# An AdaLN block and a quantised two-layer network on one core: b1 loaded as two rows, filling products in the prologue, and new orders on every engine

## The reference

```python
# conditional part, x: (2, 1024, 256), cond: (2, 128)
w_down = down_project * (cond @ down_gamma)[:, None, :] + (cond @ down_beta)[:, None, :]
w_up   = up_project   * (cond @ up_gamma)[:, None, :]   + (cond @ up_beta)[:, None, :]
y = relu(x @ w_down) @ w_up + x

# quantised network, F = 1024
def bitlinear(x, w, b):
    xq = act_quant(rmsnorm(x))     # 8 bits, one scale a token
    wq = weight_quant(w)           # -1, 0, 1 times mean(abs(w))
    return xq @ wq.T + b
h = gelu(bitlinear(y, w1, b1))
out = x + bitlinear(h, w2, b2)
```

## Time and profile before

| | us |
|---|---|
| median of 3 runs | 77.22 |
| lowest and highest run | 75.25, 78.56 |
| the profiled execution | 75.27 |
| its span (first to last instruction) | 73.5 |
| TensorE, VectorE, ScalarE, POOL busy | 63.8, 58.1, 55.1, 56.5 |

### The profile page before, as it was taken

The page is one execution under the profiler, slowest core; times in us unless marked ns, Lnnn a source line. Parts: engine busy times, 40 slices in busy tenths (PEclk is TensorE's granted clock), DMA queues, the critical chain, the costliest instruction groups (busy, mean ns, idle before and its releaser), DMA issues.

```text
span 73.5 us, 1375 instructions
## 1 busy us (share of the span) xinstructions
PE 63.8 (87%) x412; PEld 34.9 (47%) x412; DVE 58.1 (79%) x126; ACT 55.1 (75%) x113; POOL 56.5 (77%) x134
## 2 busy tenths in 40 slices
PE   3449995798999999999999999998969998699950
PEld 1042534442733422554355574834416757598830
DVE  4104357998199999799999999999999699999550
ACT  0060157994499949889999999999999999995300
POOL 6700098998889896888879899888899999899700
PEclk9999999955999999999999999999999999999998
DMA  0899999999904004436737709797997996530352
GB/s 6 263 351 288 379 406 430 419 406 428 406 40 92 16 0 89 90 58 123 133 65 143 143 15 270 147 89 167 222 198 145 181 271 118 167 143 16 144 205 73
DMA packets 20478, 13.49 MB, mean 184 GB/s; under 512 B 17748, under 2 KB 18260, under 8 KB 20088
## 3 DMA queue, kind: packets, MB, share of 16 engines
q1 hardware_dynamic: 20256, 12.69, 64.2%
q10 hardware_dynamic: 216, 0.73, 2.9%
HBM read 7.02 MB, written 2.10 MB: 124 GB/s over the span
## 4 chain that ended last, share of the span: by engine, by line
PE 51%; POOL 12%; ACT 11%; DMA 8%; DVE 7%; issue 5%; ACTq 2%; DVEq 0%; POOLq 0%
PE h L325 14%; PE ob L360 12%; DMA b1f<-b_rows 8%; ACT junk_g L481 6%; PE up_ps L302 5%; PE h L333 5%; PE up_ps L293 5%; ACT g L476 5%; POOL b1f L864 3%; DVE q L654 3%; PE ob L252 3%; PE ob L358 2%; POOL b_high L861 2%; PE up_ps L344 2%; ACTq L493 2%
## 5 line engine op out<-in xcount | busy, mean ns | idle before, releaser
L633 DVE TENSOR_REDUCE gtop<-g 128x1 f32<-128x1024 f32 x16 | 19.2, 1207 | 0.7 <-ACT g L476 0.7
L476 ACT ACTIVATE g<-h,ydeq 128x1024 f32<-128x1024 f32 x16 | 17.8, 1127 | 0.2
L481 ACT ACTIVATE junk_g<-g 128x1024 bf16<-128x1024 f32 x16 | 17.1, 1081 | 0.0
L325 PE MATMUL h<-w1q,q1t 128*128 128x512 f16 x64 | 16.5, 380 | 0.0
L360 PE MATMUL ob<-w2q,q2t 128*128 128x256 f16 x128 | 16.3, 272 | 0.0
L360 PEld LDWEIGHTS ob<-w2q,q2t 128*128 128x128 f16 x128 | 12.5, 98 | 1.4
L654 DVE TENSOR_SCALAR q<-g,gm 128x1024 f16<-128x1024 f32 x16 | 11.8, 750 | 0.1
L852 POOL TENSOR_TENSOR x<-x,b 128x512 f32<-128x512 f32 x8 | 10.1, 1271 | 0.0
L325 PEld LDWEIGHTS h<-w1q,q1t 128*128 128x128 f16 x64 | 5.6, 97 | 7.0 <-issue 2.8
L661 DVE SCALAR_TENSOR_TENSOR x<-ob,gdeq,x 128x256 f32<-128x256 f32 x16 | 7.5, 478 | 1.4 <-PE ob L360 1.4
L462 ACT ACTIVATE q<-up_ps,ym 128x256 f16<-128x256 f32 x16 | 6.8, 481 | 0.4 <-DVE ym L629 0.4
(11 more groups left out here) (104 smaller groups left out, 102.6 us busy)
## 6 DMA issues: line engine op xcount, KB each, us to landing
w<-w_t SPq DMA_DIRECT2D x4, 512.0 KB, 7.7
x<-x_tok SPq DMA_DIRECT2D x2, 1024.0 KB, 13.1
out<-x SPq DMA_DIRECT2D x7, 256.0 KB, 2.3
xd<-x_dim SPq DMA_DIRECT2D x1, 1024.0 KB, 13.0
pk<-first_pack ACTq DMA_DIRECT2D x1, 640.0 KB, 4.2
xd<-x_dim SPq DMA_DIRECT2D x1, 512.0 KB, 9.5
xd<-x_dim SPq DMA_DIRECT2D x1, 256.0 KB, 7.6
out<-x SPq DMA_DIRECT2D x2, 128.0 KB, 1.7
```

What stands on the lines that cost most here:

```text
L325: pe.matmul(h_ps[s][:, cols], q1t[:, j, s * DK + c, :], w1q[:, c, cols], start=(i == 0), stop=False)
L476: a.activation(g[:, j % RING, s, :], h_ps[s][:, :], ACT.Gelu, scale=ydeq[:, j, s:s + 1])\
L481: a.activation(junk_g[:, j % 3, s, :], g[:, j % RING, s, :], ACT.Square, scale=F ** -0.5, accum_out=gmean[:, j, s:s + 1]).then_inc(gsq_don ...
L633: v.tensor_reduce(gtop[:, j, s:s + 1], g[:, j % RING, s, :], AX.X, ALU.max, apply_absolute_value=True)\
```

## The change

Four things.

1. **b1.** The host gives b1 as two rows of 512. One load (ACT's queue, first in it) brings them to `b1`, 2 x 512. `spread_b1`, a 2 x 128 pattern of ones that POOL makes early (one memset, one copy), is the stationary operand of a 32-bit product `spread_rows`, which puts the rows on their partitions in `ob[:, 0]`. `split_b1` is now VectorE's and reads that PSUM tile; it stands between VectorE's `down_weights` and `up_weights`. The memset of `b1f` and POOL's `split_b1` are gone.
2. **Loads.** `first_pack` is issued by SP right behind `down_pack`, no longer by ACT.
3. **Filling products.** `keep_warm` calls in the prologue go from 11 products to 18.
4. **Orders.** The lists of all five engines are changed. `gelu(j, s)` for j of 4 and more now also waits for `square_g` and `quantise_g` of the pair that used its place in the ring. POOL's functions can work on several pairs at once (`CHAINS`), but every chain holds one pair; `BY_POOL` is empty, so every `quantise_g` stays on VectorE.

```diff
 LAST = PAIRS - 1
+CHAINS = [(0, 1), (1, 2), (2, 3), (3, 4), (4, 5), (5, 6), (6, 7), (7, 8)]
+CHAIN_OF = [n for n, (a, b) in enumerate(CHAINS) for k in range(a, b)]
+BY_POOL = []
...
         w2s = sb("w2s", [P, D], F16)
+        b1 = sb("b1", [2, HALF])
...
 
             sp.dma_start(dpk[:], down_pack).then_inc(dpk_in, 16)
...
+            sp.dma_start(pk[:], first_pack).then_inc(pk_in, 16)
             for k in range(DK):
                 sp.dma_start(w1[:, k], w1_t[:, k]).then_inc(w1_in[k], 16)
...
+            turn_q2(0, 1)
             turn_q1(3)
-            turn_q2(0, 1)
             turn_q1(4)
             turn_q2(1, 0)
+            store(0)
+            turn_q1(5)
             turn_q2(1, 1)
             turn_q2(2, 0)
-            store(0)
-            turn_q1(5)
             turn_q2(2, 1)
-            turn_q1(6)
             store(1)
             turn_q2(3, 0)
+            turn_q1(6)
             turn_q2(3, 1)
+            store(2)
+            turn_q2(4, 0)
             turn_q1(7)
-            turn_q2(4, 0)
             turn_q2(4, 1)
             turn_q2(5, 0)
-            store(2)
+            store(3)
             turn_q2(5, 1)
-            store(3)
...
+                pe.wait_ge(spread_set, 2)
+                pe.wait_ge(b1_in, 16)
+                pe.matmul(ob[:, 0, :], spread_b1[:, :], b1[:, :], start=True, stop=True).then_inc(b1_spread, 1)
 
             def up_weights():
...
             down_weights()
-            keep_warm(2)
+            spread_rows()
+            keep_warm(1)
             up_weights()
             down(0)
             x_tokens(0)
+            keep_warm(1)
             up(0)
             keep_warm(3)
             down(1)
+            keep_warm(2)
             weight_sum(0)
+            keep_warm(3)
             x_tokens(1)
             up(1)
             keep_warm(3)
             down(2)
             transpose_q1()
+            keep_warm(2)
             x_tokens(2)
+            up(2)
             weight_sum(1)
-            up(2)
             first_layer(0, 0)
+            first_layer(0, 1)
             column_sums()
-            first_layer(0, 1)
             x_tokens(3)
...
+            sum_w2()
             first_layer(2, 0)
-            sum_w2()
             first_layer(2, 1)
             x_tokens(5)
             up(5)
+            second_layer(0, 0)
+            second_layer(0, 1)
             first_layer(3, 0)
-            second_layer(0, 0)
             first_layer(3, 1)
             x_tokens(6)
             up(6)
             first_layer(4, 0)
-            second_layer(0, 1)
+            first_layer(4, 1)
             second_layer(1, 0)
-            first_layer(4, 1)
             x_tokens(7)
             up(7)
             second_layer(1, 1)
-            second_layer(2, 0)
             first_layer(5, 0)
             first_layer(5, 1)
+            second_layer(2, 0)
             second_layer(2, 1)
+            second_layer(3, 0)
             first_layer(6, 0)
             first_layer(6, 1)
-            second_layer(3, 0)
-            first_layer(7, 0)
             second_layer(3, 1)
             second_layer(4, 0)
+            first_layer(7, 0)
+            second_layer(4, 1)
             first_layer(7, 1)
-            second_layer(4, 1)
             second_layer(5, 0)
             transpose_q2(6, 0)
+            transpose_q2(6, 1)
             second_layer(5, 1)
-            transpose_q2(6, 1)
             transpose_q2(7, 0)
...
                 a.wait_ge(ffn1_done, SLOTS * j + s + 1)
                 if s == 0:
-                    a.wait_ge(ydeq_done, j + 1)
+                    a.wait_ge(ydeq_done, CHAIN_OF[j] + 1)
+                if j >= RING:
+                    a.wait_ge(gsq_done, SLOTS * (j - RING) + s + 1)
+                    g_quantised(a, j - RING, s)
                 a.activation(g[:, j % RING, s, :], h_ps[s][:, :], ACT.Gelu, scale=ydeq[:, j, s:s + 1])\
                     .then_inc(gelu_done, 1)
...
-            a.dma_start(pk[:], first_pack).then_inc(pk_in, 16)
-            a.wait_ge(b1_zero, 1)
-            for r in range(4):
-                a.dma_start(b1f[32 * r + 1:32 * r + 10, :], b1_rows[r % 2]).then_inc(b1_in, 16)
+            a.dma_start(b1[:], b1_rows).then_inc(b1_in, 16)
             a.preload_act_table(ACT.Gelu)
             relu(0)
             absolute_sum(0)
             square_y(0)
             relu(1)
             quantise_y(0)
+            round_weights(0)
             absolute_sum(1)
-            round_weights(0)
             square_y(1)
             quantise_y(1)
...
             square_y(2)
             gelu(0, 0)
             quantise_y(2)
             gelu(0, 1)
             square_g(0, 0)
-            relu(3)
+            round_weights(1)
             square_y(3)
             quantise_y(3)
+            relu(3)
             gelu(1, 0)
             gelu(1, 1)
             square_y(4)
+            quantise_y(4)
             gelu(2, 0)
-            quantise_y(4)
             square_g(0, 1)
             gelu(2, 1)
+            square_g(1, 0)
...
             quantise_y(5)
             gelu(3, 0)
-            square_g(1, 0)
+            square_g(1, 1)
             gelu(3, 1)
-            square_g(1, 1)
             square_y(6)
...
+            square_g(3, 1)
+            gelu(5, 1)
+            square_g(4, 0)
             quantise_y(7)
-            gelu(5, 1)
-            square_g(3, 1)
-            square_g(4, 0)
+            square_g(4, 1)
             gelu(6, 0)
-            square_g(4, 1)
+            gelu(6, 1)
             square_g(5, 0)
-            gelu(6, 1)
-            gelu(7, 0)
             square_g(5, 1)
             square_g(6, 0)
+            gelu(7, 0)
             square_g(6, 1)
             square_g(7, 0)
...
+            def split_b1():
+                v.wait_ge(b1_spread, 1)
+                v.wait_ge(part_set, 5)
+                for n, rows in enumerate((ob[:, 0, :], b1f[:, :])):
+                    if n:
+                        v.wait_ge(b1_rest, n)
+                    v.tensor_scalar(b1_high[:, :], upper_half(rows), part[:, n:n + 1], 0.0, ALU.mult, ALU.add)\
+                        .then_inc(b1_upper, 1)
+                    v.wait_ge(b1_upper, n + 1)
+                    v.tensor_tensor(b1f[:, :], rows, b1_high[:, :], ALU.add).then_inc(b1_rest, 1)
...
             v.memset(warm[:], 0.0).then_inc(warm_set, 1)
-            v.memset(b1f[:], 0.0).then_inc(b1_zero, 1)
             v.memset(part[:], 0.0).then_inc(part_set, 1)
...
             down_weights()
+            split_b1()
             up_weights()
```

190 lines of the change are left out of this document (102 added, 88 removed).

## The result

The changed kernel took 79.44 us (median of 4 executions, 78.44 to 106.13) against 77.38 for the kernel before, executed beside it. The ratio is 1.043, with a 95% interval of 1.029 to 1.058: slower. The profiled execution of the changed kernel took 78.81 (span 77.0), that of the kernel before 75.27 (span 73.5).

The account below looks back on a forecast made before the run. Bound: a prologue of waits to 20 us (b1f's load, POOL's split), then full engines. Gains of 1.7 at 20 us, 1.4 at the last gelu, about 1.5 at the end: 75.7 on the median's footing, forecast 75.3, range 73.1 to 77.5.

Parts of the forecast that it names:

- The loads: Start of the prologue: down_pack lands at 3.0 instead of 4.62, and b1 at 3.
- spread_rows: TensorE's prologue: the added 32-bit product of 512 columns takes 0.9 us and is done at 4.9.
- TensorE's own queue ahead of up(0): Prologue: wu ready at 8.4 to 8.6, gain 0.8 us, with the seven more filling products lying in TensorE's waits.
- The gain at 20 us: End of the prologue: first_layer(0, 0) starts at 18.5 against 20.2, a gain of 1.7 us.
- The clock: TensorE from 14.9 to 18.3: fillers hold the clock at 1.00 instead of 0.50, saving 1.0 us on down(2), just hidden.
- rival 2: Whole kernel: the clock spreads the runs, and slower ones vanish with TensorE busy from 3 us; 73 to 74.8, chance 0.22.
- Passes through full engines undiminished: Main part: what is won ahead of 20 us reaches the end through the full engines without loss.
- SP's order: Main part, SP's queue: stores hold back transposes behind them, but turn_q1(7) comes about 52, no later than quantise_y(7) allows.
- POOL's order: Main part, POOL's queue: with b2's additions and chain_g(3) ahead, inverse_y(7) ends near 53, when turn_q1(7) is due.
- ScalarE between 20 and 40: Sign of being right: ScalarE's idle time there stays about as now, 1.6 us.
- signs named as wrong the last: Main part: last gelu under 0.7 us earlier though first_layer(0, 0) is 1.7 us earlier, so new orders lose the prologue's gain.
- The slower rival: Prologue: b1 lands late and delays up_weights and down(0); landing at 6.7 gives 78.3, 1.1 us slower; chance 0.10.
- rival 3: Half the gain is lost to a fixed down_pack time, a falling clock or new waits; 76.4 to 77.3, chance 0.23.

Follow-up runs that it names:

- g11: The kernel before with first_pack issued by SP behind down_pack and seven more filling products, nothing else; 77.12 us in one execution.
- h17: The same kernel as e4, measured again in five rounds; 74.73 us, ratio 0.993 to the kernel before.
- e4: The kernel before, all five lists as they were, with the new b1 path, first_pack on SP and the 18 filling products; 75.96 us.
- f7: The changed kernel with turn_q2(1, 1) ahead of store(0) and turn_q1(5), and add_b2(5), add_b2(6) and chain_g(3) behind inverse_y(7); 76.33 us.
- h15: f7 measured again in five rounds; 76.10 us, ratio 1.014 to the kernel before.
- h13: f7 with the prologue's order swaps on TensorE, ScalarE, VectorE and POOL undone too; 75.55 us, ratio 1.002 to the kernel before.
- g10: f7 with the old path of b1, four loads on ScalarE's queue and the split on POOL; 76.90 us.
- h18: h13 with add_b2(4) moved behind chain_g(3) and add_b2(7) moved behind chain_g(4); 75.89 us.
- e1: The changed kernel with POOL's whole list as in the kernel before; 80.04 us.
- e3: The changed kernel with both POOL's and SP's whole lists as in the kernel before; 80.97 us.
- f6: The changed kernel with only add_b2(5), add_b2(6) and chain_g(3) moved behind inverse_y(7) on POOL; 78.24 us in one execution.
- h14: h13 with sum_w2 back behind first_layer(2, 0) and quantise_y(4) back behind gelu(2, 0); 78.67 us, ratio 1.048.

## Why the prediction was wrong

It said 75.3, with 0.07 for slower by over 2%. Step by step:

- **The loads: right.** down_weights start at 2.84 (3.0 predicted), b1 is no wait.
- **spread_rows: mis-sized.** The term was 0.9 us, half of L235's 1.79 for "four instructions (two products)"; it took 2.07. The misreading is of the overlap. The views by line give the duration of each instruction, spread_rows and then up_weights of the changed kernel, then up_weights of the kernel before:

```profile
L251 PE MATMUL ob<-b,spread_b x2: 1056/1137/1218, 4.0 to 5.0; 2*128 2x512 f32 x2
```
```profile
L256 PE MATMUL h<-pk,dpk x4: 1061/1089/1117, 6.5 to 7.5; 128*64 128x512 f32 x4
```
```profile
L235 PE MATMUL h<-pk,dpk x4: 874/996/1116, 6.6 to 7.5; 128*64 128x512 f32 x4
```

  One instruction of 512 columns takes about 1.1 us in the changed kernel, in both places. But the two products of up_weights are each 64 columns of the array wide (128*64) and run side by side, so four instructions take the time of two; spread_rows is 128 wide (2*128) and stands alone, so its price was the 1.79 of the whole row, not half of it. The rest is the clock: all of this ran at the lower level, and only L235's second half had left it. The filler right behind spread_rows, at 6.00, lasts 0.61 us, and up_weights' 1.98 us for 4 instructions of 512 columns is what down(2) took for 8 of 256 at a granted clock of 0.50; at 1.00 the same down(2) takes 1.08.
- **TensorE's own queue ahead of up(0): left out of the sum.** `wu` came at 9.61 instead of 8.5 (the split took 2.7, not 2.4), but up(0) started only at 10.38. The prediction put the seven new fillers into waits; one stands in front of up(0). And it took the clock of the kernel before for everything up to 11 us, while down(0) and x_tokens(0), now begun at the lower level, cost 0.75 us more. square_y(0) ended at 12.70 instead of 11.0, 1.7 late; POOL's chain behind it took 4.3 us instead of 5.1 and ends at 17.04 (16.1), relu(2) at 18.08 (17.0), first_layer(0, 0) starts at 19.56 (18.5). The 1.5 us from relu(2) to it were right to the tenth. The gain at 20 us was 0.6, not 1.7. One program spreads over 0.7 us here (19.14 to 19.87 above), so part of this is the execution's luck.
- **The clock: right.** 1.00 from 14.9 to 18.3, and down(2) takes 1.08 instead of 1.98. g11 shows that it could have gone otherwise. That it rises late in the first 10 us was not foreseen. The runs did not come down to the best of before, so rival 2's time is out.
- **"Passes through full engines undiminished": right in h17** (0.81, 0.81, 0.80, 0.80), not in e4, the same program, where a lead of 1.02 was gone at the end.
- **SP's order: the step that failed.** The prediction wrote "each store waits for a combine, so it holds back the transposes behind it", and then worked out one transpose, turn_q1(7). It did not put a time on turn_q2(1, 1) behind store(0) and turn_q1(5). From the trace of the kernel before this could be had: inverse_y(5) ends at 42.8, turn_q1(5) holds the queue for 1.2 us, and a q2 transpose lands 3.1 us after its issue, near 47.1, while second_layer(1, 1) was due at 45.89. That is about 1.2 us of the 2.44; the rest is the longer hold of the queue by turn_q1(5), which nothing in the prediction's rows foretold.
- **POOL's order: the step that failed next.** "That one ends near 53" was for inverse_y(7); it ended at 58.10. The new list puts add_b2(5) and add_b2(6) (1.27 each), chain_g(2) (2.0) and chain_g(3) (1.8) in front of it, 6.3 us in all. None of them waits for anything: POOL's view of waits between 38 and 60 is empty, it is simply busy. They were not added up along POOL's queue, though the prediction had named three of them; the sum is the delay of 5.5 us (52.60 to 58.10) and more. Behind inverse_y(7) stood turn_q1(7) and two q2 transposes.
- **ScalarE between 20 and 40: right**, 1.46 us idle against 1.64. Of the signs named as wrong the last is the one that came, in kind: the last gelu 2.03 later though first_layer(0, 0) is 0.6 earlier.
- **The slower rival** was a late b1. The true one, a queue's head that holds back what is ready, had no case of its own; rival 3's "a new order waits where I saw none" was capped at 77.3 for no reason that a row gave.

The account from 78.63 down to 75.2, by means: 2.4 us for the two places (f7 and h15, 76.21), 0.65 for the prologue's orders (h13, 75.55), 0.2 for the remaining orders (e4 and h17, 75.35). The new path of b1 gives 0.7 (g10), which is inside all of these. Only the first term is clear of the spread: e4 and h17, one program, differ by 1.2 in their means. Open: whether and by what path the prologue's orders cost time, and whether it is the packet of the instruction queue that makes turn_q1(5) late.

## What to carry to other kernels

When a call is moved in a fixed queue, write down for each call behind it when its data is ready, and when everything now in front of it can be issued; the largest difference is the price, and it may lie on another engine than the move. Lists tuned together are one object: test single places, never one engine's whole list, and expect that closing one of two holes shows nothing. A lead won early is real, but see what it will fall on later. When a price is read off a row of several instructions, look whether they ran side by side, and at which clock level. And let one program be measured twice before half a us between two programs is explained.

## What the hardware showed that was not expected

A quantise_g of VectorE that starts while POOL's add_b2 is running ends 0.55 us after it, wherever it began: 38.26 to 39.33 with add_b2 ending at 38.77 and 44.42 to 45.65 with 45.10 in f7, 59.43 to 61.12 with 60.57 in e4, 57.99 to 59.20 with 58.65 in h18, and in the changed kernel the worst, 1.72 us:

```profile
47.21 1.72 DVE L691 TENSOR_SCALAR q<-g,gm 128x1024 f16<-128x1024 f32 x1
...
47.11 1.27 POOL L902 TENSOR_TENSOR x<-x,b 128x512 f32<-128x512 f32 x1
```

So it is in all profiles that have the whole add_b2, without an exception in the 40 cases where it began more than 0.19 us before the add_b2's end. It does not run slower, it stands still: the 0.55 us are less than its own 0.74, and do not depend on how long it stood. The Trainium skill (SBUF — State Buffer, SBUF: two separate sides) says that VectorE and GpSimd share one pair of ports under an exclusive lock, held for a whole instruction, and that the other blocks fully; the trace agrees, with these five pairs.

It holds the other way round too, and there it costs POOL. POOL's gdeq (L876), 0.20 us when alone, takes 0.59 when a quantise_g is in its way, in the changed kernel:

```profile
56.01 0.74 DVE L691 TENSOR_SCALAR q<-g,gm 128x1024 f16<-128x1024 f32 x1
56.21 0.59 POOL L876 TENSOR_TENSOR gdeq<-grms,gstep 128x2 f32<-128x2 f32 x1
```

An add_b2 that starts in a quantise_g lasts 1.72 to 1.81 us instead of 1.27 (ten cases, in e1, e3, f6, f7, g10, h13, h14 and h15). The profiled mean of quantise_g tells it before any timeline does: 750 ns in the kernel before, 859 after.

One and the same program can fall on either side of such a hit. e4 and h17 are word for word the same, start first_layer(0, 0) 0.2 us apart (19.14 and 19.35) and end 1.8 us apart in their profiles; the earlier one is the slower. The moment at which TensorE reaches its higher clock level in the prologue is one of the things that differ: x_tokens(0) takes 0.66 us in e4 and 0.83 in h17.
